# Edge columns made inside the first CompGCN pass, with the source indices turned first

## The reference

```python
for l in range(2):
    comp = x[src] * rel_emb[l][ridx]
    agg_f = segment_sum(comp * norm * fmask, dst, num_segments=N)
    agg_b = segment_sum(comp * norm * bmask, dst, num_segments=N)
    x = relu(agg_f @ w_fwd[l] + agg_b @ w_bwd[l] + x @ w_loop[l])
```

## Time and profile before

| what | value |
| --- | --- |
| median of three runs | 7978.98 us |
| the profiled execution, its own time | 7989.64 us |
| its span | 7987.8 us |
| POOL busy | 5549.5 us, 69% of the span |
| PE busy | 4741.7 us, 59% |
| DVE busy | 3864.4 us, 48% |
| ACT busy | 1868.9 us, 23% |
| granted TensorE clock, mean | 0.694 |

### The profile page before, as it was taken

How to read it: one execution, slowest core, us unless ns; L and a number is a source line. 1 busy time by engine, 2 the same in 40 slices (tenths; PEclk the granted TensorE clock), 3 DMA queues, 4 the chain that set the end, 5 groups by cost and what they waited for, 6 DMA issues and landing times. The chain is left out here.

```text
span 7987.8 us, 125448 instructions
## 1 busy us (share of the span) xinstructions
PE 4741.7 (59%) x34986; PEld 3948.8 (49%) x34987; DVE 3864.4 (48%) x11822; ACT 1868.9 (23%) x4889; POOL 5549.5 (69%) x5840
## 2 busy tenths in 40 slices
PE   2544554333356656567777767777666666666665
PEld 2544443333344444445555545555455555566665
DVE  5444432222242111157777757777566666444444
ACT  1333331111112222222222222222222222111111
POOL 3777766777747777737777567777477777377776
PEclk7777775555667777767778878878855555666666
DMA  4666652222223333335555455555344444244443
GB/s 127 194 196 191 198 152 78 77 78 79 78 66 93 92 92 92 88 107 168 167 167 166 121 160 166 167 166 167 97 116 115 115 115 115 77 132 131 131 131 100
DMA packets 730163, 1012.26 MB, mean 127 GB/s; under 512 B 358264, under 2 KB 399288, under 8 KB 729752
## 3 DMA queue, kind: packets, MB, share of 16 engines
q1 hardware_dynamic: 516328, 550.62, 22.9%
q0 software_dynamic: 213552, 458.86, 21.6%
HBM read 912.10 MB, written 96.87 MB: 126 GB/s over the span
## 5 line engine op out<-in xcount | busy, mean ns | idle before, releaser
L849 POOL DMA_INDIRECT gat_rows<-xw_table,gat_index x2496 | 2361.7, 946 | 1047.0 <-issue 724.8
L2127 PE MATMUL bank<-gat_msg_s,gat_hot 128*128 128x264 f32 (+1 forms) x4992 | 1612.6, 485 | 175.6 <-DVE acc L2049 126.7
L2127 PEld LDWEIGHTS bank<-gat_msg_s,gat_hot 128*128 128x128 f32 x4992 | 1164.8, 274 | 453.4 <-DVE acc L2049 202.2
L898 PE MATMUL bank<-gcn_msg_s,gcn_hot 128*128 128x128 f32 x3328 | 639.7, 371 | 685.8 <-DVE acc L908 661.9
L849 POOL DMA_INDIRECT att_rows<-pre_table,att_index x832 | 785.9, 945 | 364.5 <-issue 246.8
L849 POOL DMA_INDIRECT gcn_rows<-in_x,gcn_index x832 | 808.6, 972 | 300.0 <-issue 249.3
L849 POOL DMA_INDIRECT msg_rows<-pre_table,msg_index x832 | 787.9, 947 | 328.7 <-issue 252.0
L849 POOL DMA_INDIRECT gcn_rows<-x_table,gcn_index x832 | 797.5, 958 | 306.6 <-issue 253.2
L898 PEld LDWEIGHTS bank<-gcn_msg_s,gcn_hot 128*128 128x128 f32 x3328 | 608.8, 282 | 713.9 <-DVE acc L908 575.6
L1092 PE MATMUL bank<-gcn_rel,gcn_rhot 100*128 100x128 f32 x1664 | 314.2, 366 | 536.3 <-DVE gcn_rhot L1038 536.3
L2028 DVE TENSOR_TENSOR gat_msg_s<-gat_rows,bank 128x2112 f32<-128x2112 f32 (+1 forms) x312 | 622.9, 1996 | 7.1 <-ACT bank L1937 0.6
(11 more groups left out here) (325 smaller groups left out, 8533.3 us busy)
## 6 DMA issues: line engine op xcount, KB each, us to landing
gat_hot_half<-edge_hots SPq DMA_DIRECT2D x312, 256.0 KB
gat_dhot<-dst_hots SPq DMA_DIRECT2D x312, 256.0 KB
gcn_dst<-dst_rows SPq DMA_DIRECT2D x104, 512.0 KB, 7.1
gcn_ids<-rel_rows SPq DMA_DIRECT2D x104, 400.0 KB
gat_rows<-xw_table,gat_index POOLq DMA_INDIRECT x2496
edge_hots<-gcn_hot_half SPq DMA_DIRECT2D x104, 256.0 KB, 2.2
dst_hots<-gcn_dhot SPq DMA_DIRECT2D x104, 256.0 KB, 3.5
next_rows<-gcn_coming SPq DMA_DIRECT2D x104, 256.0 KB
```

The costliest lines, as they stand in the source:

```text
L849: pool.indirect_dma_start(self.rows[n.q][:, j, :], None, self.table, bass.IndirectOffsetOnAxis(ap=self.index[n.q][:, j:j + 1], axis=0))\
L898: ins = pe.matmul(place(banks, g, width), hot[:, j, :], msg[:, j, 0:width], start=j == tiles[0], stop=j == tiles[-1])
L2127: ins = pe.matmul(bank_of(n, g)[:, 0:wide], hot[n.q][:, j, :], msg[q][:, j, :], start=j == n.groups[g].start, stop=j == n.groups[g].stop - 1)
```

## The change

`edge_columns` and `load_nodes` are no stages of their own any more. A class `EdgeColumns` holds their tiles and semaphores, made in the stage of the first pass, and its methods are put at the head of each engine's program in that pass. The source array is turned by itself, into two PSUM banks of its own, as soon as its conversion is done; ACT copies it out, and brings the index tiles of the first four steps before it enters its pipeline. The other four arrays are turned through four banks after the last row operation. The node features are loaded by SP at the end of its program. SP waits for the row tables to be written before it loads from them.

```diff
         sort_edges(nc, m, a)
-        edge_columns(nc, m, a)
-        load_nodes(nc, m, a)
...
+class EdgeColumns:
...
+        self.src_ps, self.rest_ps = m.ps[0:2], m.ps[2:6]
+    def store(self, sp):
+        sp.wait_ge(self.ready, 1)
...
+        sp.wait_ge(self.wrote, 48)
+    def load_nodes(self, sp):
...
+    def fetch(self, pool):
...
+    def keep_src(self, act):
+        for i, (k, size) in enumerate(self.columns):
+            act.wait_ge(self.src_turned, i + 1)
+            act.activation(self.m.src_i[:, k * P:(k + size) * P], self.src_ps[i][:, 0:size * P], ACT.Copy).then_inc(self.src_kept, 1)
+        act.wait_ge(self.src_kept, len(self.columns))
+    def make(self, dve):
...
+        dve.memset(m.x[:, N // P, :], 0.0).then_inc(self.zeroed, 1)
+        dve.wait_ge(self.edges_in, 16 * KT)
+        dve.wait_ge(self.counted, 1)
+        then(dve.tensor_copy(src[:, :, :], field(0)))
+        then(dve.tensor_copy(dst[:, :, :], field(1)))
...
+            for bank, t in zip(self.rest_ps, (m.dst_l, m.w_fwd, m.w_bwd, m.run_end)):
...
+    def turn(self, pe):
+        pe.wait_ge(self.step, 1)
+        for i, (k, size) in enumerate(self.columns):
+            for j in range(size):
+                ins = pe.transpose(self.src_ps[i][:, j * P:(j + 1) * P], self.src[:, k + j, :], self.m.ident[:, :])
+            ins.then_inc(self.src_turned, 1)
+        pe.wait_ge(self.ready, 1)
...
+        pe.wait_ge(self.src_kept, len(self.columns))
+        pe.wait_ge(self.kept, len(self.columns))
...
+def behind_first(count, part):
+    return lambda n: None if n.turn is None and n.ahead == 0 and n.r < count else part(n)
...
         if first:
+            columns = EdgeColumns(nc, st, m, a)
...
             def _(pool):
+                if first:
+                    columns.fetch(pool)
                 g.program(pool, comp_made)
...
+                    columns.store(sp)
                     pipeline(sp, (0, load_ids), (0, load_dst), (3, store_hots))
                     load_gcn_weights(sp, m, a, layer)
+                    columns.load_nodes(sp)
...
+                    columns.keep_src(act)
+                    bring = g.bring_index(act)
+                    for r in range(RING):
+                        bring(Step(None, r))
                     act.wait_ge(negated, 1)
-                    pipeline(act, (0, g.bring_index(act)), (0, edge_to_dst), (1, take), (1, widen))
+                    pipeline(act, (0, behind_first(RING, bring)), (0, edge_to_dst), (1, take), (1, widen))
...
                     dve.sem_inc(rel_hot, RING)
+                    columns.make(dve)
...
                 if first:
+                    columns.turn(pe)
                     pe.wait_ge(rel_loaded, 32)
```

More of the change, by code:

```diff
@@ L445, in _ @@
                 ins.then_inc(turned, 1)
[L448 to L535, removed]
```

80 lines of the change are left out of this document (65 added, 15 removed).

## The result

The changed kernel takes 7939.78 us (median of 5 runs, 7922.01 to 7946.47) against 7979.53 us of the kernel before in the same comparison (5 runs, 7976.99 to 7986.49): a ratio of 0.994, 95% interval 0.9929 to 0.9951, 39.8 us off. Forecast were 37.7 us off and 7941.3. In a second comparison it was 7937.16 against 7982.89 (ratio 0.9937, 0.9923 to 0.9951).

A forecast was written before the change was run, and what follows sets the result against it. POOL's unbroken string of 832 gathers was taken to bound the first pass, its end moving with its first gather. 39.2 - 1.5 - 0 - 0 = 37.7 us off the 7978.98 median gave 7941.3 us, range 7930 to 7958.

The forecast's parts named there:

- Part 1: Head of first pass: source column turned and index brought early; first gather at 75.4 us, 39.2 us earlier.
- Part 2: First 32 gathers: DVE row operations now beside them hold some up; about 1.5 us later, bounds 0 and 8.
- A full lock over all row operations: First gathers: DVE row operations lock POOL out wholly, costing 8 us; sum then 31.2 us off, or 7947.8.
- Part 3: Pipeline behind first gathers: ACT's step 4 index tile at about 115.6 us, in time for gather 33; cost 0, bounds 0 and 8.
- Part 4: End of first pass: SP's node load there is covered by 10 us; cost 0, bounds 0 and 3.
- The sum: Whole kernel: 39.2 - 1.5 - 0 - 0 = 37.7 us off, 7941.3 us against the median; chance 0.82.
- all later stages would shift by the same amount: Stages behind the first pass: a sign of being right, each shifted equally; last gather 37 to 38 us earlier.
- The late index: Rival at gather 33: POOL waits up to 8 us for step 4's index tile; 7942 to 7950, chance 0.10.
- the pass was not POOL's alone: Rival, first pass: PE, ACT and DVE set its end, 14.3 us earlier; 7964.7; chance 0.05 with "not as it says".
- The slower case, the clock: Rival, stages between passes: TensorE's clock falls to its lower level, 44 us more in one stage; chance 0.03.
- The small shifts of this kind: Stages between passes: small clock shifts, up to 10 us either way, put into the range.

The follow-up runs named there:

- The two experiments that eat up the margin: Against the changed kernel: `acc` cleared behind the row operations, 7939.83 us; first fetched column converted, turned and brought by itself, 7939.88 us.

## Why the prediction was right

**Part 1, first gather 39.2 us earlier.** 39.5 measured (75.07 against 75.4). Each hand-over was a little shorter than 0.1 us, and the clearing was hidden as said. The experiment without the head start confirms that the time follows this gather: 21.1 us later, 19.5 us slower.

**Part 2, 1.5 us lost to DVE.** 1.9 measured in the four gathers named above, and gather 33 at 117.79 against 117.7. A gather that comes up in a DVE instruction with two SBUF inputs stands until its end: line 521 ends at 75.93 and the gather of 75.07 at 76.75, 0.82 us behind it, as in the earlier trace rows. The Trainium skill's rule ("SBUF — State Buffer", "Who interferes with whom") on such instructions holds by these rows. The same section infers that a `tensor_tensor` leaves descriptor generation alone; by these rows it does not (1.68 us instead of 0.94 under line 521), and the measurement decides. A full lock over all row operations is refuted: of the 9 us only 1.9 were lost, because a gather that is already under way is not stopped by such an instruction (the one at 77.06 took 0.94 us, though line 525 began at 77.09). I had put all row operations down as having two inputs in SBUF, which is wrong for line 530 (514 before): it has one, and held the gather at 79.56 all the same, as the `tensor_scalar` of line 1057 holds gathers in the whole pass.

**Part 3, index tile in time, cost 0.** Right. The row tables were in DRAM sooner than I put it, first id load at 91.03 and not 92.3, while the chain behind took 0.8 us longer than said up to the composition, at 105.10 (105.6), and 0.2 from there to the tile, at 115.28 (115.6). The 1.5 us that I had put for the last completion are shown by no run; the load went out 0.2 us behind the 90.8 at which I had the traffic end. The two experiments that eat up the margin, one from each side, show the wait that I had named as next.

**Part 4, node load at the end, cost 0.** Right behind the last gather, where it is 0.1 us at most. A cost before it would drown in the differences between first passes of the same code.

**The sum.** 37.7 forecast, 39.8 and 45.7 measured in two comparisons. The mechanism was right, and that the number came so close is partly luck, for two things that I had not in the sum stand against each other. The last gather of the first pass came 35.1 us earlier in one profile and 36.6 in the other, where I had written 37 to 38. From step 4 on the pass of the profile after loses another 2.5 us: 1140.4 - 117.8 = 1022.6 us for the gathers from 33 on, 1020.1 before. In the second profile of the changed kernel they took 1020.2, so this is not a fixed cost of the change; 2.3 of the 2.5 us are time in which gathers were held. Against that, the profile after gains 8.2 us in the second pass, and the medians leave 3 to 11 us (39.8 and 45.7, less 36.6 and 35.1) that came from behind the first pass.

So the step that did not hold is that all later stages would shift by the same amount. The change does nothing in them, but how often a gather is held depends on how it and the DVE instruction fall together, and this differs by up to 24 gathers a pass. Whether the 24 of the profile before are usual for that kernel at this level was not shown; its execution was 10.1 us slower than the median, and against the median they may be no gain at all.

**The rivals.** The late index did not come (margin 1.5 us) but was only that far away. That the pass was not POOL's alone is refuted at this level by the experiment without the head start. The slower case, the clock, did not come; the mean granted clock was 0.694 before and 0.697 after. The small shifts of this kind that I had put into the range did come: the stage behind the second pass took 76.45 us at a granted clock of 0.57 before, and 78.1 to 83.9 in the nine other profiles at this level, at 0.56 down to 0.50, the longest at the lowest.

## What to carry to other kernels

Where one queue feeds a pass without a gap, bring its first entry forward, and look up by how many entries it may lead and what it needs for the entry behind these: here a lead of four steps, 1.5 us of margin, and behind it a tile that an engine brought later than it could. Price work that is moved beside POOL's gathers by its instructions with two SBUF inputs, one gather each at most, and by `tensor_scalar` operations from SBUF to SBUF like `relation_hot`, which here held even a gather that began up to 0.5 us before them. If an instruction with two SBUF inputs comes in every step, put one of its inputs into PSUM by an idle engine. And look first at what holds gathers already: here that was `relation_hot`, with 22.8 us in the first pass, about half of what the whole change brought, and no run has tried to move it. A median that moved by less than the first gather did, as where the node load alone was moved, calls for a profile of the later passes before a reason is given.

## What the hardware showed that I had not expected

In the second pass of the eight kernels that leave it as it was, the held gathers come in numbers of 1 to 24 in 104 steps, 0.5 us each, and whether one is held turns on hundredths of a microsecond. They are one of three things that make a stage longer or shorter which the change does not touch. The others are pauses of POOL in the graph-attention passes, none in one profile and 12 us in one pass of another, whose cause is open, and the granted clock in the stages between the passes, as far as the rows show it.

The same kernel took 7980 us in the first comparisons and 10534 and 10594 in the last two, with PE standing between its own matmuls for 529 us in the first pass. What made PE stand was not shown.
